# A ternary feed-forward's weights made in pieces during the attention in front of it, and the passage between the two re-ordered

## The reference

```python
def _weight_quant(w):
    scale = 1.0 / jnp.clip(jnp.mean(jnp.abs(w)), 1e-05)
    return jnp.clip(jnp.round(w * scale), -1.0, 1.0) / scale
def _act_quant(x):
    scale = 127.0 / jnp.clip(jnp.max(jnp.abs(x), axis=-1, keepdims=True), 1e-05)
    return jnp.clip(jnp.round(x * scale), -128.0, 127.0) / scale
...
x = x + tanh(g_xattn[0]) * L0_xattn(layernorm(x), ctx, ctx)   # 16 heads of 16, two softmaxes, o normalised per head
x = x + tanh(g_ffn[0])   * L0_ffn(layernorm(x))               # bitlinear(silu(gate) * up), inner size 1024
x = x + tanh(g_xattn[1]) * L1_xattn(layernorm(x), ctx, ctx)
x = x + tanh(g_ffn[1])   * L1_ffn(layernorm(x))
```

## Time and profile before

| | |
|---|---|
| median of 3 timed runs | 1340.4 us (1339.28 to 1341.74) |
| the profiled execution | 1340.51 us, span 1338.4 us |
| first attention | to about 677 us |
| passage, from the last maxima | 658 to about 720 us |
| first feed-forward | sequence 0 from 685 us, to about 930 us |
| second layer | from 930 us |
| busy: PE, DVE, ACT, POOL | 1206.9, 1116.8, 1020.4, 847.1 us |

### The profile page before, as it was taken

One profiled execution on the slowest core, in us unless ns is written; L12 is line 12 of the kernel. 1 busy time (PEld: TensorE's weight loads), 2 busy tenths in 40 slices (PEclk: granted clock), 3 DMA queues, 4 the chain that ended last, 5 costly groups with the idle time before them and its releaser, 6 DMA issues.

```text
span 1338.4 us, 30930 instructions
## 1 busy us (share of the span) xinstructions
PE 1206.9 (90%) x11672; PEld 853.6 (64%) x11672; DVE 1116.8 (83%) x1824; ACT 1020.4 (76%) x1741; POOL 847.1 (63%) x1320
## 2 busy tenths in 40 slices
PE   4699999999999999999968999995799889389898
PEld 3377777777777777777634566664667667244476
DVE  3488988998898889988868999983647999989898
ACT  2287888888888878888747999996455766699897
POOL 2157686867778687777783888865016686878000
...
GB/s 153 110 155 122 143 138 145 143 128 158 126 151 134 144 141 124 129 125 121 114 1 1 1 2 1 1 1 45 184 134 125 113 160 94 0 263 303 37 406 375
DMA packets 124963, 165.70 MB, mean 124 GB/s; under 512 B 47362, under 2 KB 78210, under 8 KB 120450
## 3 DMA queue, kind: packets, MB, share of 16 engines
...
...
## 4 chain that ended last, share of the span: by engine, by line
PE 49%; DVE 15%; POOL 14%; ACT 12%; issue 6%; DMA 3%; SPq 1%; ACTq 0%; DVEq 0%; POOLq 0%
PE psum L591 8%; PE psum L606 7%; PE psum L578 4%; PE psum L566 4%; ACT f_gelu L2160 4%; PE psum L1045 3%; PE psum L636 3%; PE psum L618 3%; POOL rs L911 3%; ACT f_gelu L2152 3%; PE psum L1080 2%; PE psum L543 2%; POOL a_fac L1861 2%; PE psum L553 2%; PE psum L1540 1%
## 5 line engine op out<-in xcount | busy, mean ns | idle before, releaser
L719 ACT ACTIVATE exp_t<-psum 128x512 f32<-128x512 f32 x512 | 278.8, 600 | 103.3 <-PE psum L591 103.3
L791 DVE TENSOR_REDUCE neg_max<-psum 128x8 f32<-128x1024 f32 x256 | 312.8, 1222 | 31.7 <-PE psum L578 24.0
L911 POOL TENSOR_TENSOR rs<-rs,minus_half 128x16 f32<-128x16 f32 x64 | 187.9, 2935 | 5.0
L591 PEld LDWEIGHTS psum<-q_stack,k_stack 50*128 50x128 f32 x2048 | 133.4, 186 | 75.8 <-ACT exp_t L719 41.6
L591 PE MATMUL psum<-q_stack,k_stack 50*128 50x128 f32 x2048 | 169.6, 285 | 1.4 <-ACT exp_t L719 1.4
L606 PE MATMUL psum<-exp_t,v_pad 128*32 128x256 f32 x2048 | 137.1, 385 | 0.7 <-ACT o_nt L729 0.4
L578 PE MATMUL psum<-k_stack,q_stack 48*128 48x256 f32 x1024 | 119.1, 310 | 18.5 <-DVE neg_max L791 15.3
L1045 PE MATMUL psum<-f_w,f_xqt 128*128 128x512 bf16 x512 | 125.3, 388 | 8.5 <-DVE f_hid L1197 3.4
L106 DVE BATCH_NORM_STATS2 norm_stats<-x_state 128x6 f32<-128x256 f32 x256 | 102.2, 413 | 27.3 <-POOL x_state L1284 15.8
L903 POOL TENSOR_TENSOR sq<-u 128x256 f32<-128x256 f32 x64 | 39.3, 615 | 109.0 <-DVE u L812 109.0
L1861 POOL TENSOR_TENSOR a_fac<-a_fac,a_expo 128x16 f32<-128x16 f32 x16 | 52.8, 3301 | 83.5 <-DVE a_fac L1767 83.1
...
## 6 DMA issues: line engine op xcount, KB each, us to landing
k_stack<-k_hi SPq DMA_DIRECT2D x252, 128.0 KB, 4.3
...
k_stack<-k_lo SPq DMA_DIRECT2D x126, 128.0 KB, 4.5
...
```

What stands on the lines that cost most here:

```text
L591: r = e.matmul(psum[:, 2 + j, o:o + P], self.k_st[rows, b // 2 % self.NK, pair // 2 % 2, pair % 2, i, pair // 4, b % 2, :], self.q_st[rows ...
L719: e.activation(self.prob[:, n % 3, j].rearrange("p n w t -> p (n w t)"), psum[:, 2 + j, :], ACT.Exp).then_inc(s["exp"], 1)
L791: e.tensor_reduce(self.negm[:, b % 2, :, :, 2 * u:2 * u + 2].rearrange("p j w n -> p j n w"), psum[:, 0:2, :].rearrange("p j (n w k) -> p ...
L911: e.tensor_tensor(self.rs[:, i], self.rs[:, i], self.expo[:, :], ALU.pow).then_inc(s["pool"], 1)
```

## The change

The ternary weights are no longer made from whole weights in the passage. Each weight is cut into two halves of 1024 columns, six pieces in all. The first attention takes them through one piece's room of 128 x 1024 f32 (and one of bf16), twice. First round: SP loads a piece in sequences 7, 9, ..., 17 (u = 6), ACT sums its absolute values in 8, 10, ..., 18 (u = 5). At tick 162 PE adds over the partitions, for all three weights at once, into bank 4; ACT copies the means; PE's max_rows(19), which writes the same bank, waits for the copy; DVE makes the scales at tick 169. Second round: SP loads a piece in sequences 23, 27, ..., 43 (u = 6); DVE rounds, clamps and writes it as bf16 in the three sequences behind (u = 4 each); SP stores it to DRAM one sequence later (w_scratch). At ticks 500, 508 and 516 SP loads the finished bf16 weights, 512 KB each.

The last transposed scores (n = 249, 251, 253, 255) go to banks 0 and 1, which the maxima have left. So scores_t(n) waits for the exponentials of step n - 2 there and no longer for those of n - 1, from n = 249 on.

The tables are new: DVE takes the token maxima at ticks 512, 513, 518 and 524; POOL has three places in a sequence for work of the feed-forward and quantises sequences 0 to 7 in the attention's last ones; gate_up(0) stands at tick 527, with steps 1, 2 and 3 at 530, 534 and 538. gate_up waits for the last exponential ahead of the gate projection and no longer between gate and up. RING is 6. Cut to its core:

```diff
+    PIECES = 6
+    SUM_AT, MEANS_AT, ROUND_AT = [7 + 2 * n for n in range(6)], 20, [23 + 4 * n for n in range(6)]
+    MEANS, SCALES = 1, 2
...
+        self.w16 = sb("f0_w16", [P, 3, self.W], BF16)
...
+    def load_piece(self, w, n):
+        i, h = divmod(n % self.PIECES, 2)
+        name, tiles = (("w_gate_t", 1), ("w_up_t", 1), ("w_down_t", 4))[i]
+        if n <= self.PIECES:
+            w.wait_ge(self.s["act"], n)
+        else:
+            w.wait_ge(self.s["dve"], self.ternary(n - self.PIECES - 1))
+        w.e.dma_start(self.piece.rearrange("p (c n) -> p c n", c=tiles),
+                      self.sh.t[name][tiles * P * h:tiles * P * (h + 1)].rearrange("(c p) n -> p c n", p=P)).then_inc(self.s["in"], 16)
+    def store_piece(self, w, n):
+        i, h = divmod(n, 2)
+        w.wait_ge(self.s["dve"], self.ternary(n))
+        w.e.dma_start(self.sh.t["w_scratch"][i][:, h * self.H:(h + 1) * self.H], self.piece16).then_inc(self.s["out"], 16)
...
+        w.wait_ge(self.s["out"], 16 * self.PIECES)
+        w.wait_ge(self.a0.s["st_pe"], 8 * (NSEQ // 2 - 2))
+        w.e.dma_start(self.w16[:, i], self.sh.t["w_scratch"][i]).then_inc(self.s_load[i], 16)
+    def act_sum(self, w, n):
+        i, h = divmod(n, 2)
+        w.wait_ge(self.s["in"], 16 * (n + 1))
+        w.e.activation(self.piece16, self.piece, ACT.Abs, accum_out=self.sum[:, h, i:i + 1]).then_inc(self.s["act"], 1)
...
+    def pe_means(self, w, bank):
+        w.wait_ge(self.s["act"], self.PIECES)
...
+            r = w.e.matmul(self.sh.psum[:, bank, 0:3], self.sh.ones[:, :], self.sum[:, h, :], start=h == 0, stop=h == 1)
         r.then_inc(self.s["pe"], 1)
+    def act_means(self, w, bank):
+        w.wait_ge(self.s["pe"], 1)
+        w.e.activation(self.mean[:, :], self.sh.psum[:, bank, 0:3], ACT.Copy, scale=1.0 / (256 * 1024)).then_inc(self.s["act"], 1)
+    def means_copied(self, w):
+        w.wait_ge(self.s["act"], self.PIECES + 1)
+    def dve_means(self, w):
+        self.means_copied(w)
+        w.e.tensor_scalar(self.mean[:, :], self.mean[:, :], 1e-5, None, ALU.max).then_inc(self.s["dve"], 1)
         w.wait_ge(self.s["dve"], self.MEANS)
+        w.e.reciprocal(self.scale[:, :], self.mean[:, :]).then_inc(self.s["dve"], 1)
+    def dve_round(self, w, n):
+        w.wait_ge(self.s["in"], 16 * (self.PIECES + n + 1))
+        w.wait_ge(self.s["dve"], self.SCALES)
...
+        w.e.tensor_scalar(self.piece, self.piece, self.scale[:, n // 2:n // 2 + 1], ROUND, ALU.mult, ALU.add).then_inc(self.s["dve"], 1)
+    def dve_clamp(self, w, n):
+        w.wait_ge(self.s["dve"], self.SCALES + 3 * n + 1)
+        w.e.tensor_scalar(self.piece, self.piece, ROUND - 1, ROUND + 1, ALU.max, ALU.min).then_inc(self.s["dve"], 1)
+    def dve_ternary(self, w, n):
+        w.wait_ge(self.s["dve"], self.SCALES + 3 * n + 2)
+        w.wait_ge(self.s["out"], 16 * n)
+        w.e.tensor_scalar(self.piece16, self.piece, ROUND, None, ALU.subtract).then_inc(self.s["dve"], 1)
...
+    def sp(self, w, tick):
+        b, u = divmod(tick, 8)
+        if u == 2 and b - 4 in self.ROUND_AT:
+            self.store_piece(w, self.ROUND_AT.index(b - 4))
+        for first, times in ((0, self.SUM_AT), (self.PIECES, self.ROUND_AT)):
+            if u == 6 and b in times:
+                self.load_piece(w, first + times.index(b))
+    def act(self, w, tick):
+        b, u = divmod(tick, 8)
+        if u == 2 and b == self.MEANS_AT:
+            self.act_means(w, 4)
+        if u == 5 and b - 1 in self.SUM_AT:
+            self.act_sum(w, self.SUM_AT.index(b - 1))
+    def dve(self, w, tick):
+        b, u = divmod(tick, 8)
+        if u == 1 and b == self.MEANS_AT + 1:
+            self.dve_means(w)
+        for i, step in enumerate((self.dve_round, self.dve_clamp, self.dve_ternary)):
+            if u == 4 and b - 1 - i in self.ROUND_AT:
+                step(w, self.ROUND_AT.index(b - 1 - i))
...
+    TAIL = 4 * NSEQ - 8
...
+    def score_bank(self, n):
+        return 0 if n > self.TAIL and n % 2 else 2
...
+            if b == TernaryWeights.MEANS_AT - 1:
+                self.tw.means_copied(w)
...
-            w.wait_ge(s["exp"], 2 * n)
+            if n <= self.TAIL:
+                w.wait_ge(s["exp"], 2 * n)
+            else:
+                w.wait_ge(s["max"], 4 * NSEQ)
+                w.wait_ge(s["exp"], 2 * n - 2)
+            bank = self.score_bank(n)
...
+            ahead(b, 0)
...
+            ahead(b, 1)
...
-            ahead(b)
+            ahead(b, 2)
...
+        tw.piece, tw.piece16 = hr_2[:, :], self.down_sb[:, :, :].rearrange("p i d -> p (i d)").bitcast(BF16)
...
-    RING = 4
+    RING = 6
...
-    PE_AHEAD = {529: -2, 530: -1, 532: 0, 534: 1, 537: 2, 541: 3}
-    ACT_AHEAD = {530: -2, 531: -1, 532: 0, 535: 1, 538: 2, 541: 3}
-    DVE_AHEAD = {516: -12, 517: -8, 531: -4, 532: 0, 537: 1, 540: 2, 543: 3}
-    POOL_AHEAD = {62: range(-16, -11), 63: range(-11, -8), 64: range(-8, -1), 65: range(-1, 2), 67: range(2, 3)}
+    PE_AHEAD = {522: -2, 527: 0, 530: 1, 534: 2, 538: 3}
+    ACT_AHEAD = {522: -2, 527: 0, 530: 1, 534: 2, 538: 3}
+    DVE_OPENS, DVE_AHEAD = {512: 0, 513: 4, 518: 8, 524: 12}, {530: 0, 533: 1, 536: 2, 540: 3}
+    POOL_OPENS = {(62, 2): (range(0, 5), range(0)), (63, 2): (range(5, 10), range(0)), (64, 0): (range(10, 12), range(0, 4)), (64, 1): (range(12, 16), range(0)), (65, 1): (range(0), range(4, 6)), (66, 1): (range(0), range(6, 8))}
+    POOL_AHEAD = {(66, 2): range(0, 2), (67, 2): range(2, 4)}
+    QUANTISED_AHEAD = 8
...
+        def ahead(tick):
+            self.tw.sp(w, tick)
+            if tick in (500, 508, 516):
+                self.tw.load(w, (500, 508, 516).index(tick))
...
+            w.wait_ge(a0.s["exp"], 8 * NSEQ)
             project(b, self.banks(b, 0), wg).then_inc(s["gate_pe"], 1)
             tw.wait_ready(w, 1)
-            w.wait_ge(a0.s["exp"], 8 * NSEQ)
...
-            if b == 2:
-                tw.pe_means(w, 1, 7)
...
-            if tick == 517:
-                tw.pe_means(w, 0, 0)
+            if tick == 8 * tw.MEANS_AT + 2:
+                w.wait_ge(a0.s["div"], 4 * tw.MEANS_AT - 10)
+                tw.pe_means(w, 4)
...
-            if b in (0, 1):
-                tw.act_sum_down(w, b)
-            if b == 4:
-                tw.act_round_down(w, 0)
-                tw.act_round_down(w, 1)
-            if b == 6:
-                tw.act_ternary_down(w, 0)
-                tw.act_ternary_down(w, 1)
...
+            tw.act(w, tick)
...
+        def token_group(b):
+            token_max(b)
+            if b % 8 == 4:
+                token_scale(b // 8)
...
-            if b % 4 == 0 and 0 <= b + 12 < NSEQ:
-                token_max(b + 12)
-                if b % 8 == 0:
-                    token_scale((b + 12) // 8)
-            if b == 3:
-                tw.dve_means(w, 1, 7)
-            if b == 5:
-                tw.dve_clamp_down(w, 0)
-                tw.dve_clamp_down(w, 1)
...
-            if 512 <= tick < 516:
-                tw.dve_sum(w, *divmod(tick - 512, 2))
-            if tick == 518:
-                tw.dve_means(w, 0, 0)
-            if 519 <= tick < 531:
-                i, n = divmod(tick - 519, 6)
-                (tw.dve_round, tw.dve_clamp, tw.dve_ternary)[n // 2](w, i, n % 2)
+            tw.dve(w, tick)
+            if tick in self.DVE_OPENS:
+                token_group(self.DVE_OPENS[tick])
...
+            if self.QUANTISED_AHEAD <= b + 4 < NSEQ:
...
+        def ahead(b, place):
...
+            normed, quantised = self.POOL_OPENS.get((b, place), ((), ()))
+            for n in normed:
+                normalise(n)
+            for n in quantised:
+                if n == 0:
+                    token_scale(0)
+                quantise(n)
+            for n in self.POOL_AHEAD.get((b, place), ()):
```

106 lines of the change are left out of this document (24 added, 82 removed).

## The result

Four timed runs of the changed kernel took 1331.9 us in the median (1329.8 to 1333.9), four of the kernel before on the same chip 1340.9: the ratio is 0.9934, 95% interval 0.9911 to 0.9958. The change makes the kernel faster by 0.7%, some 9 us at the medians. The profiled execution took 1333.8 us with a span of 1331.8, against a span of 1338.4 before: 6.6 us less.

A forecast was written before the change was run, and what follows sets the result against it. PE was taken to bound the first attention; in the passage waits and a low clock, then ACT from sequence 7. From 1340.4, minus 14 (passage) plus 3.9 (attention) gave 1330.3 us; range 1322 to 1339.

The forecast's parts named there:

- Eighteen DVE steps: First attention: round, clamp and ternary operations cost nothing in even sequences, 0.33 us for each of six odd clamps; 2.0 us.
- Means: First attention, once: PE adds the means and max_rows(19) waits for ACT's copy; 1.2 us in all.
- DMA: First attention: eighteen more transfers issued by SP where it only waits; 0 us, bounds 0 and 2.
- Step 1: Passage, tick 513: DVE waits for POOL's eight f_xn, delaying add(59) and PE's weighted(62, 0); costs 3.4 us.
- Step 2: Passage: after PE's 3.5 us idle, the next 3.5 us of work run at the lower clock; 1.7 us more.
- Steps 3 and 4: Passage to first gates: second bank pair removes exponential waits of 0.2 to 0.5 us each; Silu 0 at 681.
- Step 5: Passage: sequences 1 to 4 run in the shadow of attention's last normalise on POOL; Silu 5 at 700.2.
- weak-passage rival: Passage: PE idles 2 to 3 us per sequence and stays at the lower clock; gain 7, 1337 us, chance 0.08.
- Step 6: Passage, steps 5 to 11: ACT is full for 21.7 us; with 1.5 us for idle gaps, Silu 12 at 723.5.
- The wait at 513: Passage rival: harmless because POOL's f_xn come earlier or PE doesn't run dry; 4.9 us less, 1325 us, chance 0.12.
- Slower: First attention rival: no slack, every added operation delays PE by its whole length; 21.6 us, 1348 us, chance 0.08.
- Exclusion: First attention rival: DVE stands up to 2.91 us when a piece's operation meets POOL's L911; 9 us, 1339, chance 0.02.

The follow-up runs named there:

- e8: The changed kernel with ACT's six sums of magnitudes over 64 of 1024 columns, so the scale is wrong: 1330.3 us, single run.
- e7: The changed kernel with each piece's three DVE steps on 64 of 1024 columns, most weights left unrounded: 1330.9 us, single run.
- e3: The changed kernel with the pieces' DVE steps two sequences apart, all on even sequences: 1330.9 us median.
- e5: The changed kernel with the pieces' DVE steps two sequences apart, all on odd sequences: 1332.2 us, single run.
- e1: The changed kernel with DVE's token maximum over sequences 4 to 7 opened at tick 516 instead of 513, behind add(59): 1330.7 us median.
- e2: The changed kernel with nine unread matmuls added on PE at tick 516, in the idle time before weighted(62, 0): 1329.0 us median.
- e9: The changed kernel with all transposed scores, the last eight too, in one pair of banks as before the change: 1334.3 us median.
- e12: The changed kernel with token maximum behind add(59), DVE steps off sequences 5 and 6 of each eight, nine unread matmuls before project(61): 1329.1 us median.

## Why the prediction was right, and where it was off

The forecast was 1330.3 us; the profiled execution took 1333.8, the medians were 1331.9 and 1334.9. Faster was right. That the passage gains by more than the attention loses is shown by the marks (10.9 against 4.8 us), and the wait for f_xr is gone from the trace; that it is the moved work rather than the new tables that gained it was argued and not tried. The 3.5 us between forecast and profile are the attention (+0.9) and the passage (+3.0), less 0.5 of start and end. Within the passage the start of Silu 0 is 3.5 us later than forecast and the stretch to Silu 5 0.7 longer, and the stretch to Silu 12 is 1.3 shorter: terms that err in opposite directions helped the total.

- **Abs sums, 0.6:** 0.1 to 0.5 by e8, nearer to nothing.
- **Eighteen DVE steps, 2.0:** measured 2.8 to 3.2 (e7), and the mechanism was only half right. The step that failed is "it goes into 0.88 us idle: nothing" and, behind it, "at the two slots of u = 4 POOL is idle, so I add nothing". The slots I read, 308.6 and 318.3, lie in sequences 27 and 28; POOL's load changes with a period of eight sequences, and in two of the eight there is hardly an idle POOL. And a step in DVE's gap still delays the u that stands behind it by 0.66 us, and with it POOL's whole chain; the gap was judged by what follows it on PE alone. Where POOL can catch up, even steps were free (eleven of e3's eighteen), as forecast, and odd ones cost 0.1 to 0.2 where I had 0.33 (e5).
- **Means, 1.2:** right. PE waits 0.49 us for the copy, and the excess at sequence 19 is 1.10.
- **DMA, 0:** right for the changed kernel's pieces, as far as its traces show, but luckier than it looks: in e5 DVE waited 0.51 us for a piece, in e1 PE 0.80 us for a context load at sequence 37. Whether the pieces' traffic made that load late was not tried; the single trace of the kernel before has no such wait there. One excess of 0.37 us at sequence 51 goes with a context load that PE waited for (0.16 us, then 0.51 on ACT); it stays when the steps are short (e7) and is 0.1 or less in e3 and e5. Its cause stays open.
- **Step 1, the wait at tick 513:** the idle time was forecast at 3.4 to 3.5 us, from this chain; it is 3.90. But "this part of the change costs 3.4 us" is not shown: with the clock held up the passage is 60.0 us with the wait (e2) and 60.8 without (e1), and both traces hold 3.4 us of low clock, e1 at 685 and e2 at 693. At 0.4 us each that is 1.4 in e1, and 0.8 in e2 by e8; without them 59.4 and 59.2. So by this estimate the wait itself is worth nothing: POOL's chain stands behind it and is met again at project(61).
- **Step 2, the clock, 1.7:** the term that was mis-sized. I let 3.5 us of work run at the lower clock; it was 13.6 us, worth 4.9 us by e2. How long it lasts is chance: e3 and e9, with the same wait, have 6.8 us of it. The kernel before, whose low clock starts in the earlier trace rows, had 6.8 us of it behind 3.5 us of idle time: reading on to its end would have given about 2.7.
- **Steps 3 and 4, Silu 0:** 19.45 us behind the last max_rows by forecast, 22.97 in the trace, 18.09 in e2. Without the clock's 1.7 the forecast is 17.75: right to 0.3. But the second bank pair, which was to carry this stretch, carries 0.1 us (e9).
- **Step 5, Silu 0 to 5:** 19.2 by forecast, 19.94 measured. One idle time ahead of a gate projection (1.99 us for f_hid at 697.37) has the low clock behind it, 3.4 us for 0.8: e8 and e12, where the clock stayed up behind the same idle time, have 19.12. The weak-passage rival holds in that one place.
- **Step 6, Silu 5 to 12:** 23.3 by forecast, 21.99 measured. The 1.5 us added there for idle gaps were not needed.
- **The rivals.** The wait at 513 was nearly harmless as a wait, but not its echo, so 1325 came nowhere. Slower, from 14 us on: the attention lost 4.8. Exclusion: not at POOL's L911 (now L935), beside which no step of a piece ran in the changed kernel, so that the 2.91 us were never put to the test. But the two engines did hold each other in other places. POOL's short operation is held until DVE's ends (329.86 and 329.80), as the Trainium skill, SBUF — State Buffer, says of the shared GPSIMD/Vector port; and DVE's L802 is held beside POOL's L962, for some 0.5 us at sequence 33. So the mechanism that had a chance of 0.02 has a part in the 3.2 us, by smaller operations than the one I priced, and the 9 us did not come.
